# The first mixture of experts: all eight experts for every node, or rows sorted to slots for the two chosen

## The reference

```python
def _L0_ffn_ref(x, Wg, bg, W1, b1, W2, b2):      # D, E, H, K = 256, 8, 512, 2
    gate_scores = x @ Wg + bg
    _, idx = jax.lax.top_k(gate_scores, K)
    mask = jax.nn.one_hot(idx, E, dtype=x.dtype).sum(axis=-2)
    xf, mf = x.reshape(-1, Dv), mask.reshape(-1, E)
    h = jax.nn.gelu(jnp.einsum('td,edh->teh', xf, W1) + b1[None], approximate=False)
    y = jnp.einsum('teh,ehd->ted', h, W2) + b2[None]
    return jnp.einsum('ted,te->td', y, mf).reshape(Bv, Sv, Dv)
...
x = x + _L0_ffn_ref(_layernorm(x, axis=-1)[None], ...)[0]
```

## Time and profile before

| | us |
|---|---|
| median of 3 runs | 3857.48 |
| lowest and highest | 3857.24 to 3864.25 |
| the profiled execution | 3854.0 |
| its span in the trace | 3851.9 |

### The profile page before, as it was taken

How to read it: one execution, slowest core, us unless ns; L and a number is a source line. 1 busy time by engine, 2 the same in 40 slices (tenths; PEclk the granted TensorE clock), 3 DMA queues, 4 the chain that set the end, 5 groups by cost and what they waited for, 6 DMA issues and landing times. The chain is left out here.

```text
span 3851.9 us, 46754 instructions
## 1 busy us (share of the span) xinstructions
PE 2660.5 (69%) x10550; PEld 1816.4 (47%) x10551; DVE 1510.2 (39%) x3666; ACT 759.3 (20%) x2605; POOL 1889.8 (49%) x1926
## 2 busy tenths in 40 slices
PE   3249688465566556699999997677777755989900
PEld 2225587233333333576767665333333334666600
DVE  5774555656666653322222223322222233000075
ACT  0136000123322222222222221111111112222200
POOL 0000666265656554366666663366666611666602
PEclk9555555566666665799999998666666665999955
DMA  2012344132222222100000000233333311110001
GB/s 73 27 38 66 143 146 147 33 83 75 79 79 79 74 76 61 33 11 12 12 12 12 14 1 20 77 91 91 91 89 92 89 26 34 20 20 8 9 36 36
DMA packets 124782, 213.24 MB, mean 55 GB/s; under 512 B 56098, under 2 KB 82807, under 8 KB 122423
## 3 DMA queue, kind: packets, MB, share of 16 engines
q0 software_dynamic: 75808, 125.28, 13.1%
q1 hardware_dynamic: 48918, 87.37, 6.7%
HBM read 196.99 MB, written 15.52 MB: 55 GB/s over the span
## 5 line engine op out<-in xcount | busy, mean ns | idle before, releaser
L589 POOL DMA_INDIRECT a0rows<-table,a0idx x462 | 466.3, 1009 | 363.0 <-ACT a0idx L574 250.5
L589 POOL DMA_INDIRECT a1rows<-table,a1idx x444 | 420.1, 946 | 315.3 <-ACT a1idx L574 176.6
L619 PE MATMUL a1ps<-a1rows,a1w 128*128 128x256 f32 x888 | 435.5, 616 | 173.2 <-DMA a1rows<-table,a1idx 115.9
L619 PE MATMUL a0ps<-a0rows,a0w 128*128 128x257 f32 x924 | 428.3, 602 | 153.6 <-ACT a0w L789 71.4
L1053 POOL DMA_INDIRECT erecords<-k_rece x416 | 404.5, 972 | 213.3 <-issue 103.2
L881 PE MATMUL f0up<-k_xnT,f0w 128*128 x1280 | 386.0, 457 | 59.4 <-ACT f0hid L913 33.7
L1053 POOL DMA_INDIRECT records<-k_recg x288 | 301.0, 1045 | 226.1 <-POOLq L959 74.2
L1373 POOL DMA_INDIRECT gt_land<-table_gat,gt_source x281 | 265.9, 946 | 287.7 <-DVEq L1402 141.7
L619 PEld LDWEIGHTS a1ps<-a1rows,a1w 128*128 128x128 f32 x888 | 215.5, 284 | 393.2 <-issue 278.2
L619 PEld LDWEIGHTS a0ps<-a0rows,a0w 128*128 128x128 f32 x924 | 233.5, 286 | 345.8 <-issue 176.6
L891 PE MATMUL f0dn<-f0w,f0hid 128*128 128x256 f32 x1600 | 357.6, 380 | 9.2 <-issue 8.6
(11 more groups left out here) (387 smaller groups left out, 3133.3 us busy)
## 6 DMA issues: line engine op xcount, KB each, us to landing
es_ea<-in_eaT SPq DMA_DIRECT2D x16, 1664.0 KB
es_lane<-lane_row SPq DMA_DIRECT2D x16, 832.0 KB
so_rowl<-glane_row SPq DMA_DIRECT2D x32, 256.0 KB
a0rows<-table,a0idx POOLq DMA_INDIRECT x462
a1rows<-table,a1idx POOLq DMA_INDIRECT x444
erecords<-k_rece POOLq DMA_INDIRECT x416
table<-k_tbl SPq DMA_DIRECT2D x10, 650.0 KB, 3.6
records<-k_recg POOLq DMA_INDIRECT x288
```

The costliest lines, as they stand in the source:

```text
L589: pool.indirect_dma_start(rows[:, i, 0:TW], None, table, bass.IndirectOffsetOnAxis(ap=idx[:, i:i + 1], axis=0)).then_inc(gathered[i], 16)
L619: nc.tensor.matmul(sum_of(t), w[:, i, :], rows[:, i, 0:width], start=False, stop=False).then_inc(agg_done, 1)
```

## The change

The experts are computed on rows that are sorted by expert.

- **Sort edges.** SP also writes zeros over `slots_in`, a DRAM table of 34 x 256 rows of 1 KB, in pieces of 512 bytes: 17408 of them, 8.9 MB. It is SP's last DMA of that block. The end of the edge scores waits for it.
- **Gate load.** In the block that loads the gate's weights SP also issues 16 DMAs with the weights of all eight experts, 8.4 MB, which then stay in SBUF.
- **`l1`.** ACT keeps the normed rows (`xn_rows`) in place of their transpose. POOL issues 48 columns of `erecords` beside it.
- **Route** (`emit_route`, in place of `emit_top2_mask`). DVE chooses the two experts and computes each row's slot: a cumulative count per expert, with every expert starting at a multiple of 256 rows. POOL issues 24 columns of `erecords`, then 50 indirect DMAs that write 128 rows of 1 KB each into `slots_in`.
- **Experts** (`emit_routed_experts`, in place of `emit_experts`). A fixed loop over 32 slots of 256 rows (a pair of tiles). SP loads the rows, PE transposes them and multiplies them as before with 256 columns at a time, ACT and DVE copy the weights of the slot's expert out of the SBUF store once per slot (both `value_load` the expert's number into a register first), DVE adds the bias, SP stores the result in `slots_out`. POOL issues the other 344 columns of `erecords`.
- **`l2`.** POOL gathers 50 times 128 rows from `slots_out`; DVE adds each node's two rows to `k_x` ahead of each group's layer norm.
- **Batch norm and `l3`.** The last 112 columns of `records` go out here, 56 beside each.

PAIRS is (2 x 3200 + 8 x 255) // 256 = 32.

```diff
+PAIR = 2
+PAIRS = (2 * NP + NE0 * (PAIR * P - 1)) // (PAIR * P)
+LATE = 56
...
@@ emit_sort_edges, last on SP
+            blank = S.slots_in.rearrange("(p a) (h d) -> p (a h) d", p=P, d=P)
+            sp.dma_start(blank, S.zeros[:].unsqueeze(1).to_broadcast([P, blank.shape[1], P])).then_inc(S.blanked, 16)
...
@@ emit_routed_experts
         @block.sync
+            with sp.Fori(0, PAIRS // 2) as o:
+                for b in range(2):
+                    s = o * 2 + b
+                    sp.wait_ge(turned, s + 1)
+                    sp.dma_start(xg[b][:], rows_of(S.slots_in, s + 2)).then_inc(xin[b], 16)
+                    sp.wait_ge(added, (s + 2) * PAIR)
+                    sp.dma_start(rows_of(S.slots_out, s), yg[b][:]).then_inc(stored[b], 16)
...
         @block.gpsimd
+                group, k = divmod(next(issued) * PAIRS * EVENTS // (scatter.last - scatter.first) - EVENTS // 2, EVENTS)
+                if group < 0:
+                    return
+                if k < KH:
+                    pool.wait_ge(up_done, group * KH + k + 1)
+                else:
+                    pool.wait_ge(down_done, group * PAIR + k - KH + 1)
...
         @block.tensor
+                    pe.wait_ge(live1, s + 1)
+                    pe.wait_ge(xt_ready, s + 1)
+                    for m in range(KH):
+                        pe.wait_ge(hid_ready, s * KH + m + 1)
+                        for k in range(KD):
+                            ins = nc.tensor.matmul(up[m % 2][:, 0:PAIR * P], w1[b][:, k, m * P:(m + 1) * P], xT[b][:, k, :],
+                                                   start=(k == 0), stop=(k == KD - 1))
+                        ins.then_inc(up_done, 1)
+                    pe.wait_ge(xin[1 - b], o * 16 + 16 * (1 + b))
+                    turn(1 - b)
+                    pe.wait_ge(live2, s + 1)
+                    pe.wait_ge(hid_ready, s * KH + KH + 2)
+                    for j in range(PAIR):
+                        pe.wait_ge(added, s * PAIR + j + 1)
+                        for k in range(KH):
+                            ins = nc.tensor.matmul(down[j][:, 0:D], hid[b][:, k, j * P:(j + 1) * P], w2[b][:, k, :],
+                                                   start=(k == 0), stop=(k == KH - 1))
+                        ins.then_inc(down_done, 1)
...
         @block.vector
+                    e, after = expert_of(v, s), expert_of(v, s + 1)
+                    v.wait_ge(added, s * PAIR + PAIR)
+                    weights_over(after, 1 - b)
+                    turn_over(1 - b, s + 2)
+                    v.wait_ge(stored[b], o * 16 + 16)
+                    for j in range(PAIR):
+                        v.wait_ge(down_done, s * PAIR + j + 1)
+                        nc.vector.tensor_tensor(yg[b][:, j, :], down[j][:, 0:D], b2_rows[:, bass.ds(e, 1), :]..., ALU.add)
...
@@ emit_route
         @block.gpsimd
+            scatter.run(pool, lambda pool: None)
+            pool.wait_ge(placed, 1)
+            for n in range(COPIES):
+                if n >= 8:
+                    pool.wait_ge(put[n % 8], 16 * (n // 8))
+                pool.indirect_dma_start(S.slots_in, bass.IndirectOffsetOnAxis(ap=S.place[:, n:n + 1], axis=0),
+                                        S.xn_rows[:, n // 2, :], None).then_inc(put[n % 8], 16)
...
@@ build_kernel
+            first = Scatter(nc, S, "sc0", rece, erec_dram, 0, 48)
+            emit_layernorm_project(nc, S, "l1", wg, NE0, "rows", gate_scores, pool_work=..., sync_work=first.finish)
+            emit_route(nc, S, Scatter(nc, S, "sc1", rece, erec_dram, 48, 72))
+        emit_routed_experts(nc, S, A, Scatter(nc, S, "sc2", rece, erec_dram, 72, NC, S.erec_sb))
...
+            def add_experts(v, o):
+                v.wait_ge(came[o], 16 * 2 * U)
+                both = S.back[:, o * 2 * U:(o + 1) * 2 * U, :].rearrange("p (t r) d -> p t r d", r=2)
+                x_of = S.x[:, o * U * D:(o + 1) * U * D].rearrange("p (t d) -> p t d", d=D)
+                for r in range(2):
+                    nc.vector.tensor_tensor(x_of, x_of, both[:, :, r, :], ALU.add)
+                    v.drain()
...
-            emit_batchnorm(nc, S, A)
+            emit_batchnorm(nc, S, A, Scatter(nc, S, "sb0", recg, rec_dram, EARLY, EARLY + LATE))
...
+                rest = Scatter(nc, S, "sb1", recg, rec_dram, EARLY + LATE, GREC, S.rec_sb)
```

More of the change, by code:

```diff
@@ L99, in _ @@
                     v.drain().then_inc(sunk, 1)
+            if before_group is not None:
+                for o in range(OUT):
+                    group(o)
+            else:
+                with v.Fori(0, OUT) as o:
+                    group(o)
         @block.scalar
@@ L847, in _ @@
-            sp.dma_start(b2_rows[:], b2.unsqueeze(0).to_broadcast([P, n_experts, D])).then_inc(small, 16)
-            with sp.Fori(1, n_experts) as e:
-                sp.wait_ge(live1, e)
-                load(e)
-                sp.wait_ge(live2, e)
-                load2(e)
-            for scatter in beside:
-                scatter.finish(sp)
-        if beside:
-            @block.gpsimd
-            def _(pool):
-                total = sum(scatter.last - scatter.first for scatter in beside)
-                issued = itertools.count()
-                def pace(pool):
-                    wait_for_event(pool, next(issued) * n_experts * OUT * (PER + U) // total, up_done, down_done)
-                for scatter in beside:
-                    scatter.run(pool, pace)
+            for s in range(2):
+                sp.dma_start(xg[s][:], rows_of(S.slots_in, s)).then_inc(xin[s], 16)
@@ L974, in emit_batchnorm, with _ @@
+        @block.sync
+        def _(sp):
+            for i in range(8):
+                sp.wait_ge(put[i], 16 * ((COPIES - i + 7) // 8))
+            scatter.finish(sp)
+def emit_batchnorm(nc, S, A, scatter):
     sem = S.sem
@@ L988, in _ @@
             sp.dma_start(beta[:], A["bn_beta"].unsqueeze(0).to_broadcast([P, D])).then_inc(loaded, 16)
+            scatter.finish(sp)
+        @block.gpsimd
+        def _(pool):
+            scatter.run(pool, lambda pool: None)
         @block.tensor
```

286 lines of the change are left out of this document (183 added, 103 removed).

## The result

The changed kernel took **3904.72 us** (median of 4 runs, 3902.40 to 3910.63) against 3860.86 us of the kernel before (3857.24 to 3866.64): ratio **1.0115**, 95% interval 1.0095 to 1.0134. It is slower, by a little over 1%, and the interval leaves out 1. 3730 us and "faster" were forecast: both wrong.

A forecast was written before the change was run, and what follows sets the result against it. The prediction took PE's arithmetic in the experts' block as the bound, with POOL's scatters replacing it. Its terms summed to -129.5 us on 3854.0, plus 3.5 for the median: 3728, stated as 3730 us, range 3665 to 3815.

The forecast's parts named there:

- Behind that PE is always ahead: Experts' pair loop: after a 7 us wait POOL never waits for PE; 344 scatters at 1.262 us, 434 us, are the bound.
- the same step in `l1`, `l2` and `l3`: In these stages scatters or gathers run beside the engines' own work, costing only +7, +28 and +20 us.
- pairs over 13 us: Experts' loop: pairs this long, so that POOL waits for PE, would show the prediction wrong; 8.4 us of PE was estimated.
- Route: Routing block: 24 record and 50 row scatters at 1.262 us plus locks and landing, 98 us, all exposed, +92 us.
- batch norm: Batch norm: 56 scatters beside it, held up by DVE's long operations through a port lock, +30 us (7 to 34).
- the sign named for this: Experts' block: PE done by a third before the block's end, with scatters near 1.26 us and the block near 461 us.
- the -336: Experts' block: predicted saving in us, from 797 us before to 461 us after.
- Zeros: Sort edges: zero writes taken at 50 us delay the edge scores' loads, +24 us (0 to +53).
- gate load: Before `l1`: 16 more DMA issues at 0.5 us, 8 us, 2.5 of them inside an existing wait, +5.5 us.
- The clock rival: Experts' pair loop: PE granted only 1.2 GHz, products twice as long, block 549 us, total 3816 us; chance 0.14.
- The slower rival: Experts' pair loop: nothing overlaps at the low clock, 21.7 us a pair, total 3987 us; chance 0.06.
- "No lock": DVE's long sums don't hold POOL and 512-byte zero pieces move at full rate, total 3683 us; chance 0.10.

The follow-up runs named there:

- the first groups: Three groups of runs, a chip each, holding the first eleven experiments; the unchanged kernel took 3859, 3892 and 3894 us there.
- the last groups: Three groups of runs, a chip each, holding the last seven experiments; the unchanged kernel took 3507, 3504 and 3506 us there.

## Why the prediction was wrong

**The step that failed** is "Behind that PE is always ahead", and with it the same step in `l1`, `l2` and `l3`: each was costed as the longer of POOL's stream and the engines' own work. On the chips of the first groups the two do not run side by side at full pace, because what PE hands over comes late. `l1` needs 42.7 us after the end of POOL's stream, so in 60.6 us of stream it got 12 of its 55 us done; and the pairs, 253 us of work, took 499 where 344 x 1.262 = 434 was the bound. There the stream never ends early: its `pace` makes POOL wait for PE, so a slow PE draws the scatters out over the whole loop. This is the prediction's own sign of being wrong, pairs over 13 us (15.6). The sums came to 103 us for `l1`, 142 for `l2` and 126 for `l3`. The runs with POOL moved away (55.3 and 253 us) show that it is POOL's stream; those with one scatter in flight in `l1` and two in the pairs, that the stream can be there if it is thinner.

**What the trace of before could have told.** Its waits with DMA names of old stages were late signals: of the 435 counts of PE's products that it kept over the block, 222 stand more than 0.1 us behind the product. I took PE's 92% for proof that handoffs beside POOL are prompt, but it only proved that there was work to hide them. A pair is one chain of signals through ACT and DVE, so a late one soon is PE's idle time; more banks for the ups alone did not change that.

**The chips without late signals are the control.** There each step of the sum can be read without that cause. Route 101.1 us (98 predicted), experts' block 454.0 (461), `l1` +10.2 (+7), `l2` +27.8 (+28), batch norm +35.4 (+30), `l3` +25.8 (+20), start +25.8 (24 + 5.5). All are within 8 us; PE is done 190 us before the block's end, and the sign named for this was a third of the block. And still the change is -42 us there and not -127. The rest is in the block of before. It was 797 us in the first trace, late signals and all; on these chips it must be about 717 by estimate (856.9 in the kernel with two in flight, less the 140.3 us by which that kernel is longer than before; not seen directly). So the -336 was the difference between a measured block with late signals and a computed one without; here it is about -263.

**The other terms.** Zeros and gate load together +19.9 instead of +29.5, but by other shares. SP's issues get longer as they go on, so that `l1` waits 15 us longer (19.92 against 5.00), not 5.5. The first and the last of the eight loads of `w1`:

```profile
1522.02 0.43 SPq L1845 DMA_DIRECT2D k_w_all<-in_f_W  x1
...
1535.78 2.43 SPq L1845 DMA_DIRECT2D k_w_all<-in_f_W  x1
```

The zeros cost 9 us and not 24: the first edge-score product starts at 429.6 instead of 420.6, and on the later chips 10.0 us later than before. Their 17408 pieces move from 376.0 to 407.2, 8.9 MB in 31.2 us, where the middle of two rows gave 50. In the window in which the earlier trace rows have 429 GB/s the zeros have 284, at a full share of the DMA engines:

```profile
402.00:406.00 4.00, 0.00 (x0) 0.00 (x0) 4.00 (x1) 0.00 (x0) 4.00 (x1) 0.50 1.02 284
```

The Trainium skill (DMA: Bandwidth & Descriptors, section "Specifications") calls 512 bytes enough for the line rate. This trace does not agree: the pieces took 31.2 us and not the 21 that the rate of long rows gives, and they were not hidden, though that rule's time was nearer than mine. What is left of the change up to `l1` is within what the same code varies by: in four later traces of the first group, with this part unchanged, `l1` starts at 1531 to 1541 us.

Route: 24 and 50 scatters at 1.262 us, right; rows of 1 KB cost what records cost. Batch norm: right in mechanism and size. Four scatters stand beside DVE's long operations, one of them:

```profile
3089.95 6.83 DVE L1144 TENSOR_TENSOR k_agg<-k_agg,bnmean 128x6400 f32<-128x6400 f32 x1
3090.03 7.58 POOL L1178 DMA_INDIRECT records<-k_recg  x1 [0.30 <-issue]
```

It ends 0.83 us after DVE's operation, as in the earlier trace rows; the three others take 6.6 us each. `l2` without late signals cost 27.8 us, as predicted.

**The rivals.** The clock rival gave 16.4 us a pair, a block of 549 us and 3816. The pair (15.6), the block (520) and a lowered clock (0.80) are on the way to it, but its cause is not that: with POOL away the same instructions get 0.99. The slower rival, a pair in series, was priced from 17.7 us a pair on; the pair stayed under that, and it was `l1`, `l2` and `l3` that took the total over. "No lock" is refuted; the zeros were cheaper than the sum had them (9 us), but not at the full rate. Chances of 0.06 for slower and 0.92 for faster left no room for a cause that is common to all stages; each rival had been one stage's mishap.

## What to carry to other kernels

Work that is "hidden beside" an engine's stream is hidden only if the handoffs between the other engines stay prompt. Before costing a stage as the longer of two streams, read the waits of a stage in which both already run: here long waits put down to a DMA that ended long ago were late signals of PE, and they cost little only where PE had other work meanwhile. A block measured with such waits must not be compared with one computed without them. And a result within 2% may turn its sign from one chip to the next, as it did here: measure both kernels side by side, on more than one chip, before trusting it.

## What the runs showed of the hardware

- Beside POOL's indirect DMAs at one per 1.26 us, waits for PE's signals of 3 to 17 us appear on the chips of the first groups. In the pair loop 122 of 190 counts of PE's products come over 0.1 us late, none of 195 of DVE and ACT. With one in flight (one per 2.4 to 2.9 us) or at one per 2.9 us they are prompt; with two in flight (one per 1.5 to 1.6 us) they are prompt in the pairs and not in `l1`. The DMA engines' share was 0.02 to 0.15 meanwhile. Neither hardware loops nor the number of signals matters.
- On the chips of the last groups they are prompt at 1.31 us too. `a1`, which the change does not touch, takes 660 and 664 us (before, after) in the first traces and 610 (with two in flight beside its experts) and 606 on two of those chips; the kernel before 3507 us instead of 3859.
- Pieces of 512 bytes, written from SBUF to DRAM, move at 8.9 MB in 31.2 us with the DMA engines fully busy; long rows moved at 429 GB/s in the kernel before.
- Issues of 512 KB loads from SP, one after the other, grow from 0.43 to 2.43 us (`w1`) and from 0.47 to 0.71 (`w2`).
- POOL's idle 0.30 us between two indirect DMAs takes a memset of 0.11 us for nothing: the cadence stayed 1.263 us.
- A memset of 0.22 us with a drain behind it stretches POOL's idle time before a scatter from 0.30 to 1.69 us: the cadence went to 2.9 us.
